# AdaLN block on one core: two steps of the mixer's second norm moved, two tiles opened by VectorE, result additions given to GpSimd

## What is computed

```
h = _layernorm(x) * (1 + ca) + sa
q, k, v = split(_rms(h) @ w_qkv.T);  q = _rms(q);  k = _rms(k);  w = exp(k)
y = sigmoid(q) * cumsum(w * v) / (cumsum(w) + 1e-6)
u, g = split(y @ w_swiglu.T)
x = x + ga * (h + u * silu(g) @ w_out.T)                # the mixer
h = _layernorm(x) * (1 + cb) + sb
gate, up = h @ dequant_fp4(gate_up).T                   # scales per 128 input features
y = (silu(gate) * up) @ dequant_fp4(down).T
x = x + gb * y / sqrt(mean(y * y) + 1e-6)               # the feed-forward
```

## Time and profile before

| what | value |
|---|---|
| median of three runs | 2029.94 us |
| the profiled execution's own time | 2029.91 us |
| its span, first to last instruction | 2027.9 us |
| mean granted TensorE clock | 0.978 of full |
| mixer, feed-forward | to about 1418 us, from there on |
| one mixer pass; one feed-forward block | 164.7 us; 71.2 us |
| ScalarE read of an even tile (L1605) | 352 times, mean 0.686 us |
| VectorE read of an odd tile (L1772) | 352 times, mean 0.741 us |
| GpSimd `half` (L1679), `low` (L1691) | 176 times 1.489 us, 88 times 1.263 us |
| VectorE `norm_y` from SBUF (L1753) | 28 times, mean 1.330 us |
| VectorE `result` (L1764) | 32 times, mean 1.035 us |
| VectorE reciprocal of 512 columns | 3.35 us |

### The profile page before, as it was taken

How to read it: one execution, slowest core, us unless ns; L and a number is a source line. 1 busy time by engine, 2 the same in 40 slices (tenths; PEclk the granted TensorE clock), 3 DMA queues, 4 the chain that set the end, 5 groups by cost and what they waited for, 6 DMA issues and landing times. The chain is left out here.

```text
span 2027.9 us, 25283 instructions
## 1 busy us (share of the span) xinstructions
PE 1881.1 (93%) x8376; PEld 825.8 (41%) x8376; DVE 1427.0 (70%) x1805; ACT 924.6 (46%) x1421; POOL 871.1 (43%) x616
## 2 busy tenths in 40 slices
PE   4738999999999999999999999999999999999797
PEld 1213444444444444444444444444444343344242
DVE  6997687876877686786787675425657757767756
ACT  4435334424423523533442441221666676676574
POOL 0554324423523432432442331221676766767564
PEclk7869999999999999999999999999999999999999
DMA  7223012112021021010211101203301011101011
GB/s 297 81 79 124 27 39 67 59 39 66 10 83 63 17 83 53 28 61 26 66 59 38 46 22 53 79 16 113 137 22 63 4 60 63 35 28 42 0 42 63
DMA packets 66881, 119.38 MB, mean 59 GB/s; under 512 B 4720, under 2 KB 28272, under 8 KB 65264
## 3 DMA queue, kind: packets, MB, share of 16 engines
q1 hardware_dynamic: 66800, 118.40, 17.2%
HBM read 80.11 MB, written 38.27 MB: 58 GB/s over the span
## 5 line engine op out<-in xcount | busy, mean ns | idle before, releaser
L597 PE MATMUL bank<-Y,wsw 128*128 128x512 f16 x3072 | 682.8, 379 | 0.8 <-DVE late L960 0.8
L597 PEld LDWEIGHTS bank<-Y,wsw 128*128 128x128 f16 x3072 | 300.5, 98 | 365.8 <-issue 4.2
L900 POOL TENSOR_TENSOR late<-late 128x512 f16<-128x512 f32 x128 | 181.5, 1418 | 611.1 <-ACT late L750 610.3
L1772 DVE SCALAR_TENSOR_TENSOR f_A<-bank,gu_s,f_A 128x512 f32<-128x512 f32 x352 | 258.6, 741 | 181.8 <-ACT f_A L1605 174.8
L574 PE MATMUL bank<-late,wout 128*128 128x512 f16 x1536 | 352.4, 379 | 4.3 <-POOL late L900 4.3
L1679 POOL TENSOR_TENSOR f_A<-f_A 128x512 f32<-128x512 f32 x176 | 262.0, 1489 | 167.9 <-DVE f_A L1772 167.9
L1605 ACT ACTIVATE f_A<-bank,gu_s 128x512 f32<-128x512 f32 x352 | 240.4, 686 | 163.4 <-PE bank L1537 141.1
L550 PE MATMUL bank<-H,wqkv 128*128 128x512 f16 x1152 | 261.0, 385 | 41.2 <-DVE H L985 30.9
L1501 PE MATMUL bank<-f_HH,f_down_hi 128*128 128x512 f16 x704 | 266.3, 380 | 11.4 <-POOL f_HH L1691 10.4
L960 DVE TENSOR_TENSOR late<-late,bank 128x512 f32<-128x512 f32 x128 | 87.4, 683 | 252.6 <-PE bank L597 248.9
L574 PEld LDWEIGHTS bank<-late,wout 128*128 128x128 f16 x1536 | 149.7, 98 | 194.3 <-issue 19.7
(11 more groups left out here) (160 smaller groups left out, 2075.7 us busy)
## 6 DMA issues: line engine op xcount, KB each, us to landing
X<-xT SPq DMA_DIRECT2D x15, 1024.0 KB, 5.6
room<-packed SPq DMA_DIRECT2D x48, 176.0 KB, 2.4
h_scratch<-X SPq DMA_DIRECT2D x8, 1024.0 KB, 4.4
f_X<-x_scratch SPq DMA_DIRECT2D x8, 1024.0 KB, 5.4
x_scratch<-X SPq DMA_DIRECT2D x28, 256.0 KB, 2.1
h_scratch<-SQ SPq DMA_DIRECT2D x28, 256.0 KB, 2.2
outT<-f_X SPq DMA_DIRECT2D x7, 1024.0 KB, 4.2
wout<-wmodT SPq DMA_DIRECT2D x1, 4096.0 KB, 14.3
```

The costliest lines, as they stand in the source:

```text
L597: mm = nc.tensor.matmul(out[:], wsw[:, pw, k, col:col + P], Y[:, px, k, :], start=(k == 0 and pw == 0 and px == 0), stop=(k == DT - 1 and ...
L900: nc.gpsimd.tensor_tensor(UG[:, j % 2, 1, :], G, UG[:, j % 2, 0, :], ALU.subtract).then_inc(UG_low, 1)
L1772: nc.vector.scalar_tensor_tensor(a, EV[ev_bank(j, m, steps)][:], gu_s[:, which * I_T + j, g:g + 1], a, ALU.mult, ALU.add).then_inc(by_dve, 1)
```

## The change

In the mixer `n_squares` moves from behind the fifth copy (n = 4) to behind the sixth (n = 5), and `n_sqrt` from behind the tenth (n = 9), where it stood ahead of two squares of K, to behind the eleventh (n = 10). In the feed-forward, GpSimd's `add_y` moves from places 14, 17, 20 to 15, 16, 19. For blocks 1 to 7 tiles 4 and 6 of step 5 are read out by VectorE (`open_tile`, a multiplication by the scale into `A`) and no longer by ScalarE; `opened` says whose semaphore a waiter watches. `result` moves from VectorE to GpSimd, at places 31, 35, 39, 43. Behind the last block VectorE still adds the results.

```diff
-                    if n == DT and not (isinstance(b, int) and b == 1):
+                    if n == DT + 1 and not (isinstance(b, int) and b == 1):
                         n_squares(b - 2)
-                    if n == 2 * DT + 1 and not (isinstance(b, int) and b == 1):
+                    if n == 2 * DT + 2 and not (isinstance(b, int) and b == 1):
                         n_sqrt(b - 2)
...
-        ADD_Y = {14: 0, 17: 1, 20: 2}
+        ADD_Y = {15: 0, 16: 1, 19: 2}
...
-        RESULT = {35: 0, 36: 1, 38: 2, 39: 3}
-        assert RESULT.keys().isdisjoint(NORM_Y.keys())
+        RESULT = {31: 0, 35: 1, 39: 2, 43: 3}
+        OPENS = [(Y_MEAN // DT, 4), (Y_MEAN // DT, 6)]
+
+        def by_vector(b, j, m):
+            return not first(b) and (j, m) in OPENS
+
+        def opened(b, j, m):
+
+            if by_vector(b, j, m):
+                return opened_dve, len(OPENS) * (b - 1) + OPENS.index((j, m)) + 1
+            if first(b):
+                return by_act, DT * j + m // 2 + 1
+            skipped = sum(1 for o in OPENS if o < (j, m))
+            return by_act, (DT * I_T - len(OPENS)) * b + len(OPENS) + DT * j + m // 2 + 1 - skipped
...
-                        take(b, j, m, steps)
+                        if not by_vector(b, j, m):
+                            take(b, j, m, steps)
...
+            def result(b, c):
+                pool.wait_ge(res_loaded, 16 * (b + 1))
+                pool.wait_ge(y_norm, DT * b + c + 1)
+                nc.gpsimd.tensor_tensor(X[:, c, :], X[:, c, :], Y[:, c, :], ALU.add).then_inc(out_ready, 1)
...
+                if prev and place in RESULT:
+                    result(b - 1, RESULT[place])
...
+            def open_tile(b, j, m, steps):
                 which, g = m // DT, m % DT
                 dve.wait_ge(group_done, GROUPS * (I_T * b + j) + m + 1)
-                dve.wait_ge(by_act, DT * (I_T * b + j) + m // 2 + 1)
+                nc.vector.tensor_scalar(A[:, slot(j), 2 * which + g // 2, :], EV[ev_bank(j, m, steps)][:],
+                                        gu_s[:, which * I_T + j, g:g + 1], None, ALU.mult).then_inc(opened_dve, 1)
+
+            def take(b, j, m, steps):
+
+                which, g = m // DT, m % DT
+                dve.wait_ge(group_done, GROUPS * (I_T * b + j) + m + 1)
+                dve.wait_ge(*opened(b, j, m - 1))
...
-                for places, work in ((INVERT_Y, invert_y), (NORM_Y, norm_y), (RESULT, result)):
+                for places, work in ((INVERT_Y, invert_y), (NORM_Y, norm_y)):
...
+                        if by_vector(b, j, m - 1):
+                            open_tile(b, j, m - 1, steps)
                         take(b, j, m, steps)
```

More of the change, by code:

```diff
@@ L1355, in ffn @@
         scaled, H_high, H_low = map(sem, ("scaled", "H_high", "H_low"))
-        group_done, by_act, by_dve = map(sem, ("group_done", "by_act", "by_dve"))
+        group_done, by_act, by_dve, opened_dve = map(sem, ("group_done", "by_act", "by_dve", "opened_dve"))
         halves, gate_silu, hid_ready = map(sem, ("halves", "gate_silu", "hid_ready"))
@@ L1467, in sums_left @@
                 pe.wait_ge(by_dve, DT * (I_T * b + steps.start))
-                pe.wait_ge(by_act, DT * (I_T * b + steps.start))
+                pe.wait_ge(*opened(b, steps.start - 1, GROUPS - 2))
             def mean(b):
@@ L1532, in iteration @@
                             back, k = last
-                            pe.wait_ge((by_act, by_dve)[k % 2], DT * (I_T * b + j - back) + k // 2 + 1)
+                            if k % 2:
+                                pe.wait_ge(by_dve, DT * (I_T * b + j - back) + k // 2 + 1)
+                            elif j < back:
+                                pe.wait_ge(*opened(b - 1, I_T - 1, k))
+                            else:
+                                pe.wait_ge(*opened(b, j - back, k))
                         which, g = m // DT, m % DT
@@ L1553, in _ @@
             pe.wait_ge(by_dve, DT * I_T * NB)
-            pe.wait_ge(by_act, DT * I_T * NB)
+            pe.wait_ge(*opened(NB - 1, I_T - 1, GROUPS - 2))
             for c in range(DT):
```

## The result

The changed kernel takes 2014.22 us (median; 2013.64 to 2018.01), the kernel before 2029.7 us in the same comparison: a ratio of 0.9927, with a 95% interval of 0.991 to 0.9944. The gain is 15.5 us where 10.1 were forecast. The profiled execution took 2018.01 us, the longest of its kernel, with a span of 2016.2 us and a mean granted clock of 0.978, as before.

A forecast was written before the change was run, and what follows sets the result against it. TensorE, busy 93% of the span, was taken as the bound, its waits as what could be won. Mixer 1.1 + six blocks 7.2 + block 6 2.8 - tail 1.0 = 10.1 us off 2029.9: 2019.8 us, range 2012 to 2028.5.

The forecast's parts named there:

- the six ordinary blocks: Feed-forward blocks 1 to 5 and 7: 1.2 us gained in each, 7.2 us in all.
- Mixer, first move: `n_squares` behind the sixth copy: the 1.39 us stall at column group 7 goes, at no cost there.
- Second move: `n_sqrt` behind the eleventh copy: 0.88 us wait goes, but root 1.2 us later; both moves: 0 per loop pass, +1.1 us total.
- Steps 3 to 5: Feed-forward, `add_y` moved: 1.0 us wait goes, 0.43 comes in step 5, 0.19 saved at `y_square`: gain 0.75 us a block.
- Steps 5 and 6: Feed-forward, two tiles opened by VectorE: gain 0.6 us a block plus 0.12 in step 7, 0.8 us of stall left.
- Steps 7 to 10: Feed-forward, `result` on GpSimd: one 0.3 us stall goes, step 9's grows by 0.57; net loss 0.27 us a block.
- GpSimd the bound: Rival: colliding GpSimd work makes four steps of seven blocks 0.6 us longer each; 2035.2 us, chance 0.11.
- Block 6: Feed-forward block that also carries the second norm: gain 2.8 us, ends -0.5 and +7.
- Tail: End of block 7: the fourth result ahead of the last `half` loses 1.0 us, once.
- The second rival: The feed-forward hands its gain back, all its terms at the low ends: 2028.2 us, chance 0.17.

The follow-up runs named there:

- the results alone: The kernel before with only the residual's additions moved to GpSimd, at places 31, 35, 39, 43: 2025.49 us, ratio 0.9987.
- B with both mixer moves: The kernel before (B) with both mixer moves and nothing of the feed-forward change: 2029.58 us, ratio 1.0005.
- the whole feed-forward part: The changed kernel with both mixer moves undone: 2013.24 us, ratio 0.9922.
- the fourth result behind the last `half`: The changed kernel with GpSimd's fourth residual addition behind each block's last `half` instead of ahead of it: 2014.86 us, ratio 0.9931.
- both: The changed kernel with the fourth residual addition behind each block's last `half`, and the mixer's root behind the ninth copy and K's two squares: 1998.77 us.
- the first result later: Against the kernel of "both", GpSimd's first three residual additions moved from places 31, 35, 39 to 35, 39, 40: 1999.75 us, ratio 0.9852.

## Why the prediction was right, and where it was not

The sign and the range were right, and 2019.8 us was 5.6 us above the median. That 10.1 us is near the 11.7 us between the traces is luck: the six ordinary blocks gave 13.5 us for 7.2, while the mixer gave 1.3 less than forecast, block 6 0.8 less, the tail 1.6 less, and the start and the second pass took 1.0 more.

- *Mixer, first move: right.* The stall of 1.39 us is worth 1.38 us by itself, and copies 6 and 7 cost nothing.
- *Second move: right in that the root's delay eats the gain, wrong in the wait that shows it.* The root came 1.18 us later (forecast 1.2), and K's wait went. But "the 2.3 us come back as waits for `hidden` of steps 0 and 1" has the wrong engine for most of it: 1.92 us by starts are TensorE's wait for the silu of step 0, which stands on ScalarE behind the second norm's upper parts and so behind VectorE's scalings; only 0.18 and 0.61 us are waits for `hidden` 0 and 1. The forecast had no path over ScalarE. The pass comes out nearly as forecast, because `hidden` 0 and 1 are later still.
- *Second move, its size.* The step "`hidden` of step 0, which had waited only 0.20 us for TensorE" took those 0.20 us for slack that could be used up. In after the same 0.20 us stand ahead of the same instruction, now put down to VectorE's own reciprocal. So its wait on the instruction before it seems to take that long, whoever is named. The chain came 1.2 us later and not 1.0, and a pass is 0.23 us longer where 0 was forecast: 1.2 us in five passes. The last pass gave 1.04 (forecast 1.1), by luck: TensorE waits there for no `hidden` in the first steps, but 1.71 us by starts for the silu. Mixer: -0.1 instead of +1.1.
- *Steps 3 to 5: a term over-sized.* The old wait of 1.0 us went, as forecast. The new wait in step 5, put at 0.43 us, is 0.21, and the sum over the squares lost 0.4 us of waits by starts where 0.19 were counted. 1.08 us a block (1.23 in block 1) instead of 0.75.
- *Steps 5 and 6: right.* 0.67 us a block alone, forecast 0.6 + 0.12; what is left of the wait for `low` is 0.84 us, forecast 0.8. VectorE's reads take 0.75 and 0.74 us, between the bounds of 0.6 and 0.9, and cost nothing. The Trainium skill (VectorE: DVE Perf Modes, errata section) makes them 0.66 us, an estimate from its figures; the measurement decides.
- *Steps 7 to 10: collisions over-priced.* By starts, the wait at the start of step 9 grew from 0.38 to 0.57 us, a third of the 0.57 that it was forecast to grow by; the one at 1548.74 is gone as forecast, and a small one in step 8 is new, 0.16 us: +0.06 a block where -0.27 were forecast. The collisions are plain in the block's rows above. GpSimd's `half` at 1538.88 meets VectorE's `hidden`, which runs until 1539.41, and ends at 1540.53, 1.1 us behind that, where it takes 1.27 alone; VectorE's scaling at 1539.32 ends at 1541.08, 0.55 us behind `half`. Each seems to wait until the other is done, as the Trainium skill says (SBUF — State Buffer, "Who interferes with whom").
- *GpSimd the bound: did not happen.* Its results took 1.26 to 1.72 us, at most what was priced, and in those four steps TensorE waits for GpSimd nowhere in block 1.
- *Block 6: over-sized behind the second root.* Forecast 2.8, measured 1.96. Up to the matmul that waits for that root (1891.53, now 1879.50) the block is 1.82 us shorter, where 2.0 were forecast; of its waits, 1.12, 1.50, 1.47 and 2.04 us, the longest left are 1.71 and 1.46. Behind it VectorE's relief of four additions was to give 1.7 - 0.9 = 0.8 us, and gave 0.14; with the results alone it gave 0.17. The upper end of +7 counted on a dip of the clock to go. The clock is low once for 3.4 us in this block in both traces, and the dip costs nothing there: B with both mixer moves, whose feed-forward is that of before, has none, and its block 6 takes 89.99 us for 89.95.
- *Loop turn: missing from the sum.* Block 4 gained 3.70 us, 1.85 more than its neighbours. The experiment with the results alone puts this on them: VectorE's idle time at the turn was 5.19 us before and 2.69 with four instructions fewer in a block. Why the turn is shorter by more than those four were worth was not settled: in before the trace names nothing that VectorE waits for, and the later store and loads are a rival to the count of instructions. The row of before, TensorE's longest wait for `take` (2.97 us), is in none of the forecast's terms.
- *Tail: right in its mechanism, far too small.* "1.27 - 0.30 = 1.0 us lost, once" was lost: the wait grew from 1.50 to 2.39 us, and with the results alone the end is 0.94 us longer. In after another 1.7 us went to the clock.
- *The second rival's sum.* It says "all its terms at the low ends", but counts the results with -0.6 where their low end was -0.9, and block 6 with 1 where its own was -0.5. With those ends the rival would have been slower than before, at 2031.5 us.

## What to carry to other kernels

When an instruction is moved to clear a stall, ask which engines start their next work on that instruction, and price the delay of each such chain against its cover; here the forecast followed VectorE and missed ScalarE, and one of two moves made together cost all that the other won, and only running each alone showed it. Take idle time of a few tenths of a us ahead of an instruction for slack only after looking at whether the engine's own previous result could have been the releaser. And read the rows at every loop's turn and at the program's end for themselves: there a change meets covers that the repeated part doesn't have.

## What the runs showed of the hardware that was not expected

**A lower clock after a wait, but not after each.** In after and in four of the experiments (the whole feed-forward part, the fourth result behind the last `half`, both, the first result later) the last down matmuls run at the lower level for 3.4 us behind a wait of 2.1 to 2.4 us, which costs some 1.7 us beyond the wait. With the results alone the same wait of 2.39 us is there, and the clock stays up:

```profile
2005.44 0.38 PE L1515 MATMUL bank<-f_HH,f_down_hi 128*128 128x512 f16 x1 [2.39 <-POOL f_HH L1716]
```

The end took 25.71 us there and 27.40 in after. With waits of 1.16 and 1.50 us it stayed up too. In block 6 of before a dip of 3.4 us begins behind the wait of 2.04 us for the second root; in B with both mixer moves the same wait is there and no dip. What else decides stays open.

**The turn of a loop.** VectorE was idle for 5.19 us where the feed-forward's loop turns back, with nothing that the trace names to wait for, and TensorE ran out of work for 2.97 us of it. In kernels whose results are on GpSimd block 4 is 0.8 to 1.9 us longer than its neighbours, in those with the results on VectorE 2.8 to 3.3 (4.8 to 5.1 where the clock fell too). The cause is not shown.

**A collision 0.14 us wide.** An instruction of GpSimd that starts 0.14 us ahead of one of VectorE makes it take 1.67 us instead of 0.69 (the fourth result and the last `hidden` above). A free place on one engine's queue is thus worth little if it lies where the other engine's chain runs.
